# The window mask on TensorE: from two full-array products to eight products in the tile form of the scores

## What is computed

```python
for i in range(6):                                    # DEPTH
    x = attn_layer(shift_tokens(x), Wqkv[i], ...) + x # 16 heads of 64, windows of 32 tokens
    x = ffn_layer(shift_tokens(x), ...) + x
# in attn_layer, for every window of 32 queries and its 64 keys (the window before and its own):
mask = (it < jb) | (it > jb + w) | (jb == -1)
sim = jnp.einsum('bhwie,bhwje->bhwij', bq, bk2) * QK_SCALE
sim = jnp.where(mask, -jnp.finfo(sim.dtype).max, sim)
attn = jax.nn.softmax(sim, -1)
out = jnp.einsum('bhwij,bhwje->bhwie', attn, bv2)
```

## Time and profile before

| | us |
|---|---|
| median of 3 runs | 4664.48 (4661.28 to 4667.9) |
| the profiled execution | 4656.89 |
| its span, first to last instruction | 4655.1 |
| PE busy | 4075.6 (88%) |
| POOL busy | 2999.5 (64%) |
| DVE busy | 2885.5 (62%) |
| ACT busy | 2678.4 (58%) |

### The profile page before, as it was taken

The page is one execution under the profiler, slowest core; times in us unless marked ns, Lnnn a source line. Parts: engine busy times, 40 slices in busy tenths (PEclk is TensorE's granted clock), DMA queues, the critical chain, the costliest instruction groups (busy, mean ns, idle before and its releaser), DMA issues.

```text
span 4655.1 us, 164467 instructions
## 1 busy us (share of the span) xinstructions
PE 4075.6 (88%) x67239; PEld 2843.3 (61%) x67239; DVE 2885.5 (62%) x4666; ACT 2678.4 (58%) x5529; POOL 2999.5 (64%) x1858
## 2 busy tenths in 40 slices
PE   7879999999999999977999999999999995457875
PEld 4546666666666666635666666666666662245644
DVE  5766666666666666734666766666666663516751
ACT  4546666666666666634666666666666663224542
POOL 0038888788888888815888888888887882420002
PEclk9989999999999999979999999999999997578987
DMA  2013333433334333311333343333333330040004
GB/s 67 1 38 92 101 98 87 107 94 99 97 88 105 92 100 97 89 45 46 95 100 96 92 106 93 97 101 92 106 88 98 100 88 12 0 121 3 1 9 121
DMA packets 349815, 367.90 MB, mean 79 GB/s; under 512 B 58737, under 2 KB 285042, under 8 KB 348786
## 3 DMA queue, kind: packets, MB, share of 16 engines
q1 hardware_dynamic: 338834, 348.92, 29.1%
q0 software_dynamic: 2048, 4.20, 0.3%
q10 hardware_dynamic: 8160, 3.93, 0.3%
HBM read 247.12 MB, written 109.71 MB: 77 GB/s over the span
## 4 chain that ended last, share of the span: by engine, by line
PE 58%; ACT 15%; issue 7%; DVE 5%; SPq 3%; POOL 3%; DMA 1%; ACTq 0%; DVEq 0%; POOLq 0%
PE banks L325 11%; PE banks L386 7%; PE banks L309 6%; PE banks L330 5%; PE banks L369 5%; PE banks L430 4%; PE banks L292 4%; PE banks L424 3%; ACT arena L461 3%; ACT ln_rs L467 2%; SPq L726 1%; ACT arena L480 1%; PE banks L880 1%; PE banks L340 1%; PE banks L352 1%
## 5 line engine op out<-in xcount | busy, mean ns | idle before, releaser
L637 POOL TENSOR_TENSOR arena<-arena 128x512 f32<-128x512 f32 x768 | 959.6, 1270 | 527.7 <-DVE arena L566 401.0
L642 POOL TENSOR_TENSOR arena<-arena 128x1024 f32<-128x1024 f32 x384 | 905.3, 2357 | 30.1
L639 POOL TENSOR_TENSOR arena<-arena 128x1024 f32<-128x1024 f32 x384 | 907.1, 2362 | 0.0
L325 PE MATMUL banks<-w_qk,arena 128*128 128x512 f32 x1536 | 736.3, 602 | 16.2 <-DVE arena L666 10.6
L440 ACT COPY arena<-banks 128x512 f32<-128x512 f32 x384 | 224.0, 583 | 808.2 <-PE banks L386 808.2
L566 DVE SCALAR_TENSOR_TENSOR arena<-arena,banks 128x512 f32<-128x512 f32 x768 | 493.6, 684 | 311.8 <-ACT arena L474 310.4
L559 DVE TENSOR_REDUCE arena<-arena 128x8 f32<-128x512 f32 x768 | 494.2, 679 | 84.0 <-ACT arena L456 83.9
L533 DVE TENSOR_REDUCE arena<-banks 128x8 f32<-128x512 f32 x384 | 265.0, 690 | 402.3 <-PE banks L309 398.6
L456 ACT ACTIVATE arena<-banks 128x512 f32<-128x512 f32 x768 | 447.2, 595 | 84.9 <-PE banks L325 72.6
L325 PEld LDWEIGHTS banks<-w_qk,arena 128*128 128x128 f32 x1536 | 277.8, 194 | 272.9 <-issue 272.9
L386 PE MATMUL banks<-ident,arena 128*128 128x128 f32 x3072 | 428.1, 283 | 16.7 <-POOL arena L642 15.5
(11 more groups left out here) (219 smaller groups left out, 6796.0 us busy)
## 6 DMA issues: line engine op xcount, KB each, us to landing
v_rows<-arena SPq DMA_DIRECT2D x1536, 64.0 KB
arena<-v_rows SPq DMA_DIRECT2D x768, 128.0 KB
arena<-v_rows SPq DMA_DIRECT2D x768, 112.0 KB
arena<-in_moe_w SPq DMA_DIRECT2D x30, 515.5 KB, 3.8
w_qk<-in_stack_qk SPq DMA_DIRECT2D x48, 256.0 KB, 3.0
w_v<-in_stack_v SPq DMA_DIRECT2D x48, 128.0 KB, 3.2
w_o<-in_stack_o SPq DMA_DIRECT2D x12, 512.0 KB
w_w<-in_stack_w SPq DMA_DIRECT2D x12, 341.0 KB, 3.3
```

The costliest lines, as they stand in the source:

```text
L325: pe.matmul(bank(M, tile), f.sh[:, (s // G) % 2, o:o + 128], w.qk[:, g], start=True, stop=True).then_inc(S.qk, 1)
L637: nc.gpsimd.tensor_tensor(f.sined[:, :, :, half, :], x[:, :, :, 1 - half, :], sines[:, :, mine].unsqueeze(1).to_broadcast([D, GH, 4, DH // ...
L639: nc.gpsimd.tensor_tensor(rot, x.rearrange("p h t a d -> p h t (a d)"), cosines.unsqueeze(1).to_broadcast([D, GH, 4, DH]), ALU.mult).then_ ...
L642: nc.gpsimd.tensor_tensor(rot, rot, f.sined.rearrange("p h t a d -> p h t (a d)"), ALU.add).then_inc(S.rotated, 1)
```

## The change

`window_mask` now builds an array of 128 partitions by 2 tiles x 2 heads x 64 keys. Partitions 0 to 63 and 64 to 127 hold the same thing: 32 rows for the first window of a tile of four, and 32 rows for any of the other three. `M.wmask` is 256 columns wide and no longer 512, as are its load and its cast to bf16.

In `pe_stack_step` eight products take the place of two. Each takes 64 partitions of the mask (one half), picks 32 of the rows with 32 columns of the identity, streams all 256 columns, and writes 32 partitions of one bank. A `pe.sem_inc(M.s.pe_waited)` stands ahead of them.

```diff
-    m = np.zeros((D, 2, GH, KW), np.float32)
-    for p in range(D):
+    m = np.zeros((2, 2, WIN, 2, 2, KW), np.float32)
+    for w in range(2):
         for tile in range(2):
-            i = tile * 128 + p
-            w = i // WIN
-            j = (w - 1) * WIN + np.arange(KW)
-            m[p, tile, :, (i < j) | (i > j + WIN) | (j < 0)] = NEG
-    return m.reshape(D, 2 * GH * KW)
+            for q in range(WIN):
+                i, first = WIN * (w + 4 * tile) + q, WIN * (w + 4 * tile - 1)
+                j = first + np.arange(KW)
+                m[:, w, q, tile, :, (i < j) | (i > j + WIN) | (j < 0)] = NEG
+    return m.reshape(D, 2 * 2 * KW)
...
         st.wait(S.normed, u - 1)
-        mask = M.wmask[:].rearrange("p (x b k) -> p x b k", b=2, k=KW)
-        for par in range(2):
-            pe.matmul(bank(M, 4 + par, T), M.identb[:], mask[:, :, par, :], start=True, stop=False,
-                      skip_group_check=True)
+        pe.sem_inc(M.s.pe_waited)
+        for c in range(4):
+            for par in range(2):
+
+                r, o = slice(64 * par, 64 * par + 64), 64 * par + 32 * min(c, 1)
+                pe.matmul(bank(M, 4 + par)[32 * c:32 * c + 32, 0:T], M.identb[r, o:o + 32], M.wmask[r, :],
+                          start=True, stop=False, skip_group_check=True)
...
-    nc.vector.tensor_copy(M.wmask[:], M.mask_in[:, 0, :])
+    nc.vector.tensor_copy(M.wmask[:], M.mask_in[:, 0, 0:T])
...
-        M.wmask, M.cmask = sb("wmask", [D, 512], BF16), sb("cmask", [D, 512], BF16)
+        M.wmask, M.cmask = sb("wmask", [D, T], BF16), sb("cmask", [D, 512], BF16)
```

More of the change, by code:

```diff
@@ L1632, in hybrid_program @@
         binary.bv = binary.bv[:]
-        M.constants = [(M.x[:], ins["x"]), (M.ident[:], ins["ident"]), (M.mask_in[:, 0, :], ins["wmask"]),
+        M.constants = [(M.x[:], ins["x"]), (M.ident[:], ins["ident"]), (M.mask_in[:, 0, 0:T], ins["wmask"]),
                        (M.mask_in[:, 1, :], ins["cmask"]), (M.hmask[:], ins["hmask"]),
```

## The result

The changed kernel takes 4650.62 us (median of 15 runs, 4643.63 to 4657.1), the kernel before 4659.52 (15 runs beside them, 4651.92 to 4668.93). The ratio is 0.9981, 95% interval [0.9973, 0.9989]: 8.9 us less, between 5 and 13. The forecast was 25.7 us less. Most of its mechanism is in the trace, its size is not in the time.

What follows compares the result with a forecast made beforehand. PE's own work was taken to bound the kernel. Gains of 17.3 (steps 2, 4, 7), 8.2 (steps 1, 3) and 0.2 us (load and cast) sum to 25.7: 4664.5 - 25.7 = 4638.8, rounded 4639; range 4620 to 4662.

Steps and rivals of the forecast that it cites:

- What bounds the kernel: In the stack calls PE's own work bounds, some 380 of 400 us; largest PE wait is ACT's copy, 53.2 us.
- The change of form stays: Switching PE from whole-array products to 64 by 32 tiles moves ahead of the mask and still costs 0.10 us.
- The eight side by side, 0.107 to the first score: Eight mask products run at once, each streaming 0.107 us; the first score may follow 0.107 after the first mask product.
- T: Start of the last of the four L352 products' stream; first score forecast to move from 0.42 to 0.31 us after it.
- The event: Increment ahead of the mask, hidden by L352's last stream and the change of form: costed at nothing, 0.10 us without cover.
- Rival C: Four column tiles of one half take turns at the mask: first score at T + 0.64, 53 us slower, 4717; chance 0.09.
- Busy time: PE's busy time for mask plus scores goes down by 0.1 us a unit.
- Steps 5, 6 and 0 gain nothing: Outputs there wait for ACT's copy in 144 units; the whole gain turns into wait, 53 us to about 70.
- Steps 2, 4 and 7, 17.3 us: These three steps don't wait for the copy, so each unit gains 0.12 us: 144 x 0.12 = 17.3 us.
- Steps 1 and 3, 8.2 us: Copy ends 0.30 us before outputs start; one step gains 0.05, the other 0.12, 48 times each: 8.2 us.
- I take 0.01 gained: Instruction term per unit: twelve more instructions could cost up to 0.08 us or nothing; scores taken as 0.01 us faster.
- rival D: Smaller gain: steps 1 and 3 give nothing, others drift to a wait; 13 us less, 4651; chance 0.12.

Runs made afterwards that it cites:

- two_half_array: Changed kernel with the mask as two products of 64 partitions by 128 columns, using a selecting matrix, instead of eight: 4666.75 us, ratio 1.0007.
- event_alone: Kernel before with only the event (the semaphore increment) put ahead of its two full-array mask products: 4658.73 us, ratio 0.9996.
- no_mask: Changed kernel with the mask's products left out and the event kept, so scores are unmasked: 4631.22 us, ratio 0.9938.

## Why the prediction was right and wrong

- **What bounds the kernel**: right in that PE's own work does, wrong in leaving out "issue". The rows had 42.1 us of it ahead of the mask, the scores and the outputs, nearly as much as the 53.2 us of the copy, which I called the largest wait and followed up. I did not ask what "issue" is, and the sum has no term for it. The 2.4 GHz that the prediction gives to the granted clock of 1.00 is not in the earlier trace rows, and the distance of the two mask products, 0.109 us, gives 2.35 columns a ns. In the kernel before the bf16 records take 273 ns for 256 columns (L283) and 379 for 512 (L839), medians, so 256 columns more take 0.106 us, 2.4 columns a ns.
- **The change of form stays**: right. It is 0.10 us ahead of the eight products, and two_half_array, with two changes, pays it twice.
- **The eight side by side, 0.107 to the first score**: right. First mask record T + 0.20, eight records within 0.02, first score 0.12 behind, T + 0.32 where T + 0.31 was forecast. The 0.107 of the stream itself is 0.109 in the trace, the distance of the two L283 products in the median.
- **The event**: right; with it alone the first score stays at T + 0.42 (event_alone).
- **Rival C**: fell. The first score comes at T + 0.32, not T + 0.64, and eight weight loads of 89 ns start within 0.02 us, among the products of the same tiles, although four of them share each half of the partitions.
- **Busy time**: 0.092 a unit for 0.1.
- **Steps 5, 6 and 0 gain nothing**: right. Copy 53.2 to 69.3 for "about 70", in 146 units; periods the same within 3 ns.
- **Steps 2, 4 and 7, 17.3 us**: periods 0.076, 0.112 and 0.145 less, 16.0 us.
- **Steps 1 and 3, 8.2 us**: 0.043 and 0.113 less, 7.5 us, as the 0.05 and 0.12 that I gave them. Both of the distances seen in the earlier trace rows were real.
- **"I take 0.01 gained" for instructions**: this is the term that failed. Its bound was right in kind (up to 0.08 us lost) but by a wrong mechanism: I looked for twelve instructions that come in one by one, at 13 ns each (0.86 us over 64, which counts in the last record's own length; the records start 10 ns apart). The scores are not slower by it, 0.628 us to the last record's start where 0.643 was before, a little gained. Instructions come in blocks, and a unit either has a stop, of 0.15 to 2.5 us, or none. These stops were 42.5 us before and are 54.9, so the term measured 12.4 us of loss, 0.03 us a unit, where I had a gain of 0.01. With it, 25.7 - 12.4, the sum would have been 13 us; the stack calls gained 10.2 and the runs 8.9.
- **The numbers**: 4650.6 lies in the range of 4620 to 4662 and nearest to rival D (4651), but D's reason (steps 1 and 3 give nothing) is not what happened. That it lies there is in part luck of the place: at a shift of 32 the same kernel takes 4667, outside the range. For the profiled executions the account closes: -35.4 busy, +16.1 copy, +12.4 stops, +0.6 rest, -6.3.

What stays open: why there are more stops now. The mean over five places (42.3 to 58.8 us) fits twelve more instructions in a part that already held more than a block. But no_mask has four fewer than the kernel before there and 49.2 us of stops, event_alone has one event more and 43.6, and five places of the kernel before lie between 26 and 61 us. So this is argued, not shown. A rival stands beside it: PE gets through this part in less time, in no_mask most of all, and may for that reason be ahead of its instructions sooner. No run separates number and pace. That the stops are for instruction blocks is supported by the packets' times, by the same places in a second run, and by the shifts; a run with the mask's eight products and no event, which would take one instruction a unit away, was not tried.

## What to carry to other kernels

Give the "issue" waits of the bounding engine a term of their own before counting what an edit saves: an edit that adds instructions to a dense stretch can pay for its gain in stops, and any edit that changes their number moves the stops. For an edit worth under 1%, measure both kernels at several places (a few idle instructions at the start), or the place is what is measured. Where a wait is shorter than the work that could fill it, move half of that work: eight products ahead of a wait of 0.64 us brought nothing, four brought 9 to 15 us by the medians of the runs.

## What the runs showed of the hardware

- In the stack of the two kernels an idle time of PE that no semaphore ends is over 1.2 to 1.6 us after a 16 KB packet of instructions has landed (86 of 87 such stops; 1.7 to 2.7 for the 16 ahead of the mask), and the packet itself takes about 1.1 us. PE has 248 to 251 records to a packet. Such stops make 20 to 64 us of these 4650 us in the runs here, and shifting the kernel before by 32 to 192 instructions moves its time over 50 us (4635 to 4686 net).
- After a stop of 1.66 us the granted clock was 0.60 over 2.6 us, from 1.00; after two others of the same length it stayed at 1.00. At 0.50 the L328 products start 0.85 us apart, at 1.00 0.43.
- Four tiles of 64 by 32 that share their partitions, in each of two halves, start 3 ns apart with their bf16 weights: eight weight loads of 89 ns in 0.11 us (L286).
- A change of form costs 0.10 us from the whole array to 64 by 32 (0.21 from the second mask product to the first score, less 0.11) and 0.10 from 64 by 128 to 64 by 32 (0.213 less 0.109, two_half_array). An event behind whole-array products adds nothing (first score at T + 0.42 with and without it, event_alone); between products of one form it was 0.10.
- An increment of a semaphore at the start of PE's program takes about 0.15 us (64 more move L134 from 10.7 to 20.5 us, 9.8 / 64 = 0.153, and 192 reach 30.3).
